# Exponentials of every other group of heads read the scores straight from PSUM on ScalarE; first convolution tap on ScalarE; orders refitted

## What is computed

```
q1, q2 = q[:, :H], q[:, H:]; k1, k2 = k[:, :H], k[:, H:]        # 16 heads, two halves of width 8
a1 = softmax((q1 * 8 ** -0.5) @ k1.T) @ v
a2 = softmax((q2 * 8 ** -0.5) @ k2.T) @ v
attn = a1 - lam * a2                                            # then a norm and a projection
...
xc = depthwise_conv(x, 3 taps, causal) + dw_bias
xc = silu(xc @ pw_w.T + pw_b); x1 = x + xc
rw = weights of the top 2 of 8 experts
moe = sum_e rw[e] * silu(x1 @ expert_w[e].T + expert_b[e])
```

## Time and profile before

| | us |
|---|---|
| median of three runs (1378.17 to 1381.06) | 1378.75 |
| the profiled execution | 1372.59 |
| its span, first to last instruction | 1370.8 |
| TensorE busy | 1294.0 |
| VectorE busy | 1143.9 |
| ScalarE busy | 912.5 |
| GpSimd busy | 212.7 |

### The profile page before, as it was taken

How to read it: one execution, slowest core, us unless ns; L and a number is a source line. 1 busy time by engine, 2 the same in 40 slices (tenths; PEclk the granted TensorE clock), 3 DMA queues, 4 the chain that set the end, 5 groups by cost and what they waited for, 6 DMA issues and landing times.

```text
span 1370.8 us, 40709 instructions
## 1 busy us (share of the span) xinstructions
PE 1294.0 (94%) x17034; PEld 843.3 (62%) x17034; DVE 1143.9 (83%) x3060; ACT 912.5 (67%) x1743; POOL 212.7 (16%) x204
## 2 busy tenths in 40 slices
PE   6988899999999999999999999999999999899998
PEld 5665566556755566656755566656755567656755
DVE  6568999888898889988898889988898878966763
ACT  2565577667876687767876587757776576635663
POOL 1031220102301211102301112102301022101000
PEclk9999999999999999999999999999999999999999
DMA  7020011001110020001110020100100011000000
GB/s 269 11 48 33 10 40 33 3 1 33 33 33 2 2 62 24 12 1 32 33 33 2 1 56 10 34 1 22 43 18 2 2 36 14 18 1 17 2 1 16
DMA packets 22781, 35.73 MB, mean 26 GB/s; under 512 B 1992, under 2 KB 18504, under 8 KB 22344
## 3 DMA queue, kind: packets, MB, share of 16 engines
q1 hardware_dynamic: 22600, 33.14, 8.7%
HBM read 20.54 MB, written 8.39 MB: 21 GB/s over the span
## 4 chain that ended last, share of the span: by engine, by line
PE 60%; DVE 28%; ACT 6%; issue 4%; DMA 1%; POOL 1%; SPq 0%; DVEq 0%; ACTq 0%
PE bank L2184 11%; PE four L1954 5%; PE bank L1868 5%; PE bank L1741 4%; PE bank L2109 3%; PE bank L1766 3%; PE bank L2123 3%; PE bank L2087 3%; DVE qkv L1341 3%; DVE cs L1680 2%; PE four L1973 2%; PE bank L1870 2%; PE four L1766 2%; DVE stat L1256 2%; PE bank L1747 1%
## 5 line engine op out<-in xcount | busy, mean ns | idle before, releaser
L2184 PE MATMUL bank<-w_sb,cs 128*128 128x512 f32 x512 | 246.8, 601 | 0.1
L794 POOL TENSOR_TENSOR decayed<-state,pk 128x512 f32<-128x512 f32 x64 | 78.9, 1233 | 690.0 <-DVE state L1483 689.8
L2184 PEld LDWEIGHTS bank<-w_sb,cs 128*128 128x128 f32 x512 | 93.3, 190 | 89.2 <-issue 78.6
L1096 ACT ACTIVATE cs<-bank 128x512 f32<-128x512 f32 x112 | 66.9, 597 | 99.8 <-PE bank L1747 96.4
L829 ACT ACT_TABLE_LOAD x90 | 115.5, 1283 | 1.6
L1341 DVE SCALAR_TENSOR_TENSOR qkv<-pre,l_sb,qkv 128x512 f32<-128x512 f32 x144 | 104.1, 767 | 0.0
L1868 PE MATMUL bank<-hT,w_sb 128*128 128x512 f32 x192 | 92.7, 605 | 3.7 <-ACT pre L882 1.7
L1041 ACT COPY cs<-bank 128x512 f32<-128x512 f32 x114 | 66.1, 580 | 44.4 <-PE bank L2109 44.3
L1680 DVE SCALAR_TENSOR_TENSOR cs<-cs,rwt 128x256 f32<-128x256 f32 x196 | 87.8, 486 | 8.1 <-ACT cs L1096 5.0
L1566 DVE TENSOR_REDUCE pkc<-bank 128x8 f32<-128x512 f32 x116 | 74.4, 682 | 9.4 <-PE bank L2087 9.4
L1572 DVE TENSOR_TENSOR cs<-bank,pkc 128x512 f32<-128x512 f32 x116 | 74.2, 681 | 6.5 <-PE bank L2109 6.0
(11 more groups left out here) (291 smaller groups left out, 3016.3 us busy)
## 6 DMA issues: line engine op xcount, KB each, us to landing
xt<-in_x SPq DMA_DIRECT2D x8, 512.0 KB, 5.0
vscr<-qkv SPq DMA_DIRECT2D x8, 512.0 KB, 2.8
vT<-vscr SPq DMA_DIRECT2D x32, 128.0 KB, 4.5
Tm<-in_x SPq DMA_DIRECT2D x8, 512.0 KB, 4.1
out<-cs SPq DMA_DIRECT2D x8, 512.0 KB, 2.9
w_sb<-in_weights SPq DMA_DIRECT2D x1, 3656.0 KB, 19.1
rotb<-swapped SPq DMA_DIRECT2D x16, 128.0 KB, 2.3
swapped<-rota SPq DMA_DIRECT2D x16, 128.0 KB, 2.3
```

The source lines that it names most:

```text
L794: fin("dec", tt(decayed[:, :, :, :], state[:, :, :, :], eGC[:, c, :].unsqueeze(1).unsqueeze(3).to_broadcast([P, 4, G * B, DH]), ALU.mult))
L2184: mm(dst, x1T[:, k, b * TB:b * TB + TB], ew[:, k, ep * 512:ep * 512 + 512], start=k == 0, stop=False)
```

## The change

For the odd units (DIRECT) VectorE takes only the maximum, now negated, and ScalarE takes the exponential straight from the two PSUM banks: 16 instructions of 128x64, one for each group of keys, with the negated maximum as bias. The even units keep the subtraction (now an addition of the negated maximum) and one exponential of 128x1024. The softmax scale moves from the exponential into the copy of the queries. Whoever waited for VectorE's subtraction (the next scores, the transposes, the norm's sums, the last projection) waits, for an odd unit, for ScalarE's eight exponentials of that bank. The exponentials in turn wait for the maximum of their bank, and for the transposes of the unit before.

The first tap of the convolution moves from VectorE to ScalarE (tap0). The order tables of all five stages and KEEP are written anew.

```diff
+DIRECT = (1, 3, 5, 7)
...
-KEEP = {(-1, 1, "cond"): 61, (-1, 1, "db"): 9, (-1, 2, "gate", 0): 3, (-1, 2, "rot"): 4, (-1, 2, "turn1", 0): 36, (-1, 2,
...
+        1, "cond"): 3, (0, 1, "proj", 1, 0): 3, (1, -1, "pt", 2): 2, (1, -1, "pt", 4): 5, (1, 0, "z", 2): 1, (NI - 1,
...
+        def scores_read(up, u, a):
+            rank = sum(d < u for d in DIRECT)
+            if u in DIRECT:
+                up("direct", 2 * rank + a + 1)
+            else:
+                up("psub", 2 * (u - rank) + a + 1)
...
-                    fin("qx_sb", nc.scalar.copy(pair(p, qx), halves_of(bank[6][:, :])))
+                    fin("qx_sb", A(pair(p, qx), halves_of(bank[6][:, :]), ACT.Copy, scale=XSCALE))
 
                 def max_(u):
                     log_exp()
-                    up("psub", 2 * u + 2)
-                    fin("pexp", A(prob_of(j, u), prob_of(j, u), ACT.Exp, scale=XSCALE))
+                    prob = prob_of(j, u)
+                    if u not in DIRECT:
+                        scores_read(up, u, 1)
+                        fin("pexp", A(prob, prob, ACT.Exp))
+                        return
+                    depth = 2 if j == NI - 1 else 1
+                    if u >= depth:
+                        up("pt_ps", 2 * (u - depth) + 2)
+                    for a in range(2):
+                        up("high", 2 * u + a + 1)
+                        for h in range(8):
+                            at = slice(NK * h, NK * h + NK)
+                            last = A(prob[:, 512 * a:512 * a + 512][:, at], scores(j, u, a)[:, at], ACT.Exp, bias=mx[:, a, h:h + 1])
+                        fin("direct", last)
...
+                def tap0(p):
+                    up("t4", p + 1)
+                    bs = slice(2 * p, 2 * p + 2)
+                    for k in range(KC):
+                        fin("tap0", A(dcv[:, k, :].rearrange("p (b t) -> p b t", b=B)[:, bs, :], fT[:, k, bs, 0:TB], ACT.Identity, bias=L("dwb", k, k + 1), scale=L("dwk", 3 * k, 3 * k + 1)))
...
-                            highest[a] = link(red(mx[:, a, :], sc[a], AX.X, ALU.max))
+                            fin("high", red(mx[:, a, :], sc[a], AX.X, ALU.max, negate=True))
+                        return
+                    if u in DIRECT:
                         return
...
-                        ch.wait(highest[a])
-                        fin("psub", tt(prob_of(j, u)[:, 512 * a:512 * a + 512].rearrange("p (h n) -> p h n", h=8), sc[a], bc(mx[:, a, :], NK), ALU.subtract))
+                        up("high", 2 * u + a + 1)
+                        fin("psub", tt(prob_of(j, u)[:, 512 * a:512 * a + 512].rearrange("p (h n) -> p h n", h=8), sc[a], bc(mx[:, a, :], NK), ALU.add))
...
                     if t == 0:
-                        up("t4", p + 1)
-                        for k in range(KC):
-                            tap[k] = link(ts(r3(dcv[:, k, :])[:, bs, :], fT[:, k, bs, 0:TB], L("dwk", 3 * k, 3 * k + 1), L("dwb", k, k + 1), ALU.mult, ALU.add))
                         return
...
-                    up("psub", 2 * (u - depth) + 1 + a) if u >= depth else up("qx_sb")
+                    scores_read(up, u - depth, a) if u >= depth else up("qx_sb")
...
-                    up("pexp", u + 1)
+                    if u in DIRECT:
+                        scores_read(up, u, 1)
+                    else:
+                        up("pexp", u + 1 - sum(d < u for d in DIRECT))
```

More of the change, by code:

```diff
@@ new lines @@
+        -qx.0.0 d1.3 co.0 -pv.1 -ffd.1 onorm.0 cs.7.0 -pv.5 -pw.0.0 -turn6.1 z.7 -pt.4 wo.0 onorm.1 -pv.0 -moe.22
+        -pv.4 d1.7'''),
+        "dve": steps('''
+        -av.4.0 norm.3.0 +cond solve.11.0 o.1.2 -av.5.0 -av.3.0 -acc.10.1 -max.2.0 am.0 -acc.4.1 norm.3.1 -acc.10.0
+        norm.2.1 dsel.0 solve.13.1 -ln2.0.1 -max.4.1 s.0 -max.3.0 solve.3.1 am.2 solve.5.0 -av.7.0 solve.0.1 -av.0.0
+        zc.0 o.2.2 am.3 +db solve.8.1 -av.1.1 -ln2.0.0 -av.2.1 -max.3.1 solve.10.0 am.1 gsub.0 solve.12.1 norm.0 m.0
@@ new lines @@
+        -pt.9 -ffd.0 onorm.1 -pw.0.1 -sc.4.1 *gate.0 -turn5.0 +sum.0 -pt.5 -ffu.1 wo.1 wo.2 -moe.16 -sc.1.0 +sum.1'''),
+        "dve": steps('''
+        norm.0 dsel.0 -max.2.0 -max.7.1 -ln2.0.0 -acc.7.1 -acc.10.1 dsel.1 -av.2.0 -av.2.1 gsub.0 norm.1 gsub.1
+        norm.2.0 -av.7.1 -max.3.0 -av.4.1 norm.3.0 norm.2.1 norm.3.1 -acc.4.1 am.0 -av.5.0 -acc.8.1 -top.1.0 am.1 am.2
+        +cond am.3 solve.0.0 -ln3.1.1 solve.0.1 -max.3.1 solve.1.0 solve.1.1 +db solve.2.0 -av.1.0 -av.3.1 solve.2.1
+        solve.3.0 solve.3.1 solve.4.0 solve.4.1 -av.7.0 -max.7.0 solve.5.0 solve.5.1 +btr solve.6.0 solve.6.1
@@ L210 @@
-        dec.1 dec.2 kx.5 dec.3 dec.4 dec.5 kx.3 dec.6 dec.7 +spread +bv kx.1'''),
+        kx.5 kx.0 kx.2 scale.0 scale.1 kx.4 kx.6 scale.2 -ffd.1 scale.3 scale.4 dec.0 scale.5 scale.6 -ffd.0 scale.7
+        dec.1 dec.2 dec.3 dec.4 kx.1 dec.5 dec.6 +spread dec.7 +bv kx.7 kx.3'''),
     },
@@ new lines @@
+        -turn6.0 cs.7.0 cs.7.1 -ffd.0 +cond -turn6.1 co.0 co.1 -ffd.1 onorm.0 onorm.1 -ffu.0 wo.0 -ffu.1 wo.1 wo.2
+        +sum.0'''),
+        "dve": steps('''
+        -ln2.0.0 norm.0 -ln2.1.0 -top.0.0 -ln2.0.1 +db dsel.0 +cond -ln2.1.1 dsel.1 gsub.0 norm.1 gsub.1 norm.2.0
+        norm.3.0 norm.2.1 norm.3.1 -max.0.0 -max.0.1 am.0 am.1 -max.1.0 am.2 -av.0.0 am.3 solve.0.0 solve.0.1
+        +conv.0.0 -max.2.0 *rot.0 -max.2.1 -av.0.1 solve.1.0 solve.1.1 -av.1.0 solve.2.0 -max.3.0 solve.2.1 solve.3.0
@@ new lines @@
+        solve.10.0 -av.0.1 -max.3.1 solve.15.0 -max.4.0 -av.1.0 solve.15.1 +conv.1.2 -max.4.1 +cond gsub.0 +conv.0.1
+        solve.1.0 o.5.3 -av.1.1 norm.2.1 -dconv.1.0 solve.8.0 zc.3 -max.5.0 -av.2.0 am.2 -av.2.1 -max.1.1 -av.3.0
+        -av.3.1 o.1.1 -max.7.1 norm.3.0 zc.7 solve.9.1 o.1.2 -max.6.0 solve.6.0 o.1.3 solve.3.1 -max.6.1 solve.13.0
+        -av.4.0 -av.4.1 *ln1.0 +conv.0.0 -max.7.0 solve.6.1 o.2.3 norm.1 -anorm.0 -av.5.0 s.3 -av.5.1 -av.6.0 -wp.0
+        -ln3.0.0 -av.6.1 -av.7.0 o.4.0 norm.3.1 norm.2.0 o.7.3 norm.0 o.7.0 o.0.3 solve.9.0 solve.12.0 *ln1.1 -ln3.0.1
@@ L1613, in dconv @@
                         dst = r3(dcv[:, k, :])[:, bs, :]
-                        ch.wait(tap[k])
+                        if t == 1:
+                            up("tap0", 2 * p + k + 1)
+                        else:
+                            ch.wait(tap[k])
                         last = stt(dst, fT[:, k, bs, t:TB + t], L("dwk", 3 * k + t, 3 * k + t + 1), dst, ALU.mult, ALU.add)
```

444 lines of the change are left out of this document (214 added, 230 removed).

## The result

The changed kernel takes 1421.43 us (median of four, 1419.19 to 1426.51) where the kernel before took 1378.46 beside it: a ratio of 1.032, with 1.030 to 1.034 as its interval. It is slower by 43 us. I had forecast slower, by 9.5 us, with 1404 as the end of the range: the sign was right, the size was not.

The account below looks back on a forecast made before the run. TensorE, busy 94% of the span, was taken as the bound, VectorE as a second, ScalarE with room. Six steady blocks at +1.5 us, drain -3 and last stage +3.5 gave +9.5: 1378.75 to 1388 us, range 1360 to 1404.

Parts of the forecast that it names:

- Price of the exponentials: ScalarE, direct units: sixteen narrow exponentials take 3.3 to 3.8 us, taken 3.6; 2.55 us more a unit, 10.2 a block.
- Waits at the direct units less what goes: Steady block's attention: ScalarE's lateness at units 1, 3, 5, 7 costs TensorE +2.7 us; vanished waits for VectorE give -1.1.
- Unit 3: Steady block's attention: its transposes come 0.5 to 1.6 us late behind ScalarE's exponentials, taken 1.1.
- Unit 7: Steady block's attention: ScalarE's late exponentials and three instructions behind them delay TensorE 0.4 to 1.5 us, taken 0.9.
- the 1.1 that was to go: Steady block's attention: TensorE's waits for VectorE, 0.87 us ahead of unit 3's transposes and 0.26 ahead of unit 6's, vanish.
- Dummies: Steady blocks: eight added dummy matmuls on TensorE at 0.226 us each, all counted as unhidden, +1.8 us a block.
- What is given back: Steady block behind the attention: the lighter VectorE returns most of TensorE's 2.34 us idle time there, taken 1.9.
- Rival A: VectorE really held TensorE: steady blocks win 2.5 us each, the drain 5, the last stage nothing; 1359 us, chance 0.30.
- C's tail that absorbs: Rival, no change: the block's tail absorbs the attention's lateness; blocks 0, drain -3, last stage +3.5; 1379 us, chance 0.15.
- The drain: Drain block: VectorE is full in its attention, so its relief counts against eight more dummies; -3 us, bounds -5 and +2.
- The last stage: Last stage: VectorE no bound, ScalarE gets 10.2 us more, sixteen more dummies partly in waits; +3.5 us, bounds 0 and +5.
- the signs of being right: ScalarE over 50 us in attention, groups 3.3 to 3.8, TensorE waiting at units 3 and 7, 157 us blocks, shorter drain.

Follow-up runs that it names:

- wide exponentials: The changed kernel with one exponential of 128x512 a bank in odd units in place of eight of 128x64: 1401.86 us, ratio 1.018 to the kernel before.
- the small edits alone: First tap on ScalarE, negated maximum and scale in the query copy, no direct unit, orders and dummies of the kernel before: 1378.63 us, ratio 1.002 to it.

## Why the prediction was wrong, step by step

- **Price of the exponentials** (3.6 us a group, 10.2 a block): right, 3.4 us, a little under. ScalarE's share of the attention: 51.9 forecast, 52.02 measured, with two other instructions in it.
- **Waits at the direct units less what goes** (+2.7 - 1.1 = +1.6 us a block): the right kind of wait, but not its parts. At unit 1 the scores of unit 2 took 1.91 us where a pair takes 1.14, 0.8 us hidden inside the group, against 0.5. Unit 3: 0.95 us against 1.1, but I had priced the half of the scores ahead at 0.57 us, half a pair, and a half alone takes 1.13; joined, the wait is 2.07. Unit 7, 0.9 forecast: its transposes start at 579.20 without a wait. Of the 1.1 that was to go, VectorE's 0.87 ahead of unit 3 is still there with 0.41.
- **Dummies** (+1.8 us a block, unhidden): right. Taking them out gave 9.5 us of 10.8.
- **What is given back** (-1.9 a block): wrong. I let a lighter VectorE return time behind the attention. Two kernels with a lighter VectorE and wide exponentials have steady blocks of 155.30 and 156.70 us, and the small edits alone, with VectorE 1 us lighter, have them as before. Rival A (VectorE held TensorE) falls with it, and so does C's tail that absorbs: by these runs VectorE's 28% of the chain was not a path whose shortening helps. Without dummies and clock my terms made a block 0.3 us shorter (2.7 - 1.1 - 1.9), and it came out about 1 us longer: six blocks, some 8 us.
- **The step that failed: a wait costs its own length.** Each term of the sum priced a wait of TensorE by the time it lasts. The granted clock stood at 1.00 in every row that I quoted, and I noted it and put no term for it. The waits at unit 3, together with one for VectorE just ahead, take it to the low level, in a place of the block where projections follow. In the median this is by the estimate 11 to 13 us of the 43. The times of the kernel before that I had already spread over 1372.59 to 1381.06 us, a sign that something other than its waits' length moves it; its later runs show the clock going with the time, from 1.000 to 0.992.
- **The drain** (-3): wrong in sign, and the one term built on VectorE as the bound. From turn to turn of the cross attention it takes 157.8 us, before 149.0. With the wide exponentials, joined halves and no added dummies it takes 151.8, with the narrow ones 158.4, in which a fall of the clock is worth 1.7. So some 5 us of the 8.8 are plain length of the narrow exponentials, and no gain from VectorE's relief shows.
- **The last stage** (+3.5, at most +5): too small. From its turn on, 113 us against 104.1, +8.9. I had counted ScalarE's lateness and the dummies as costs that partly hide in one another. Without the added dummies and the parted halves it is longer still, 118.0, with the clock at 0.93; with the wide exponentials and none of them 107.6. So of +8.9 some 5 are length and its fillers, and 3.5 are there at the smaller length too.

In the median, then: clock 11 to 13 us, dummies of the steady blocks 9.5, delay by ScalarE in the steady blocks six times 1, so 6, and the drain and the last stage some 7 (8.8 less the fall) and 9: 42 to 45 where 43 are measured. Of the 34 us between forecast and result the clock, put at nothing, is the largest single piece; the drain (-3 against +7), what was to be given back (some 8) and the last stage (5.5) make up roughly the rest. That the sign came out right is no luck, since ScalarE did make TensorE wait; but of the signs of being right a wait at unit 7, a shorter drain and a steady block of 157 us did not come. The dummies were measured by taking them away, and the clock's part at unit 3 by filling the waits, alone and together (19 us); the others are read from single traces, and the drain's and last stage's shares hold their own dummies. Open is what holds the last stage up by 3.5 us with the wide exponentials, what decides whether a wait brings a fall, and whether the falls of the clock in the head (at 120 to 130 us in most of the profiled executions, one with the orders of before and no direct unit among them) are of the change at all. In the profiled executions shown, the changed kernel has falls there and the kernel before has none, and 7.6 of the 53.9 us between these two lie ahead of the first turn.

## What to carry to other kernels

On a kernel whose TensorE is nearly always busy, price a new wait of TensorE twice: by its length, and by a stretch at half the clock that can come behind it where waits stand close together; read the spread of the run times against the granted clock of each run before trusting a rest of idle time. Work taken from an engine that shares the chain with a full TensorE was worth nothing here, since TensorE's own work stayed, and less than nothing where the engine that took it over came later to a PSUM bank that TensorE needed back. Sixteen instructions in place of one cost their fixed part sixteen times: one exponential over a bank with one bias is the form to compare against.

## What the runs showed that I had not expected

- A kernel became 11 us faster by doing 5 us of useless work on TensorE at the right place, while eight dummies a block at other places cost 1.6 of their 1.8 us and held nothing.
- The same waits bring a fall of the clock in some blocks and not in others: in three of six with unit 3 through VectorE, in two of six with the wide exponentials.
- Half of a pair of 32-row products takes 1.13 us and the pair 1.14: the halves run beside one another when they stand together. Two rows of that kind were in the trace of before, and I had not read them.
- A wait can be hidden in a group's busy time: eight records of scores took 1.91 us in place of 1.14 without an idle time ahead of them.
- A narrow exponential with a pointer as bias, from PSUM, took 366 ns and let the next one start after 201.
